# First graph layer: a sixth own-row buffer, and own rows of tile t + 1 gathered ahead of the shared rows of tile t

## Chip, cores and metric

One NeuronCore of a Trainium2 chip runs the whole program. The metric is the device time of one execution in microseconds (us). Three runs of the kernel before gave 1579.4, 1580.0 and 1585.3 us, so its median is 1580.0 us.

## What is computed

Two graph layers over 8192 nodes with 128 features each, with a random adjacency matrix of 8192 x 8192 int32 (256 MB) in which one entry in 1024 is set, so that a node has about eight neighbours.

```python
h = jnp.maximum(_layernorm(x), 0.0)
x = x + L0(h, adj, Wq, Wk)      # attention by cosine of K and Q rows, softmax over neighbours,
                                # then 0.5 * (att @ h) + 0.5 * h
h = jnp.maximum(_layernorm(x), 0.0)
x = x + L1(h, adj, W, b_W, a_vec, b_a)   # h' = h W^T + b; leaky score e_i + e_j, softmax over neighbours, att @ h'
```

Rows without a neighbour are treated apart in both layers. If a row has more neighbours than the lists hold, a flag sends the program to a dense version of both layers; with the inputs used here it isn't taken.

## The kernel before

**Tiles and rows.** The nodes are cut into T = 64 tiles of P = 128 rows. For each row the kernel finds the list of its neighbours by reading the whole adjacency matrix once (the scan). The first K = 5 neighbours of a row are its own rows: five indirect DMAs per tile, each of which gathers one table row of 130 floats into each of the 128 partitions. The neighbours beyond five are packed over the rows of a tile into shared chunks of 128; 27 chunks serve QT = 8 tiles, three or four newly gathered per tile (`GIVEN`), again one indirect DMA each.

**The scan.** The SP queue loads the adjacency matrix in pieces of 1 MB, four per tile, into a ring of six (`RING`, line 223). A piece's slot is free when TensorE has folded it (line 1091). DVE's `extract` finds the set words of a folded tile and `decode` and `compact` make its list of neighbours. Every two tiles `compact` also counts the neighbours beyond five (line 1524), and TensorE turns the counts into offsets (line 1099).

**The loop.** After a start that prepares tables and scans the first tiles, each engine runs its own hand-ordered loop over t = -1 ... 63, and semaphores tie them together:

- DVE at step t: weights of tile t - 3 (`spill_weights`, line 1585), products of the own rows of tile t - 1 (line 1568), products of its shared rows (line 1575), `select(t)`, which writes the shared index of tile t (line 1557), then offsets, `compact`, `extract`, `finish(t - 5)`, `decode`. In late steps `select(t)` stands first every second time.
- TensorE at step t: half of the folds of the scanned tile, `weighted(t - 4)` (lines 1126 and 1128), the offsets, the other folds, `owners(t + 1)` (line 1114). `weighted` counts `s_pv` up, which frees the buffers of its tile.
- ScalarE at step t: copies of owners (line 1261), scores and exponentials of tile t - 2 (line 1279), masks of tile t + 2 (lines 1247 to 1251), diagonals of tile t - 2.
- GpSimd (POOL) only issues gathers: for each t a wait for `s_pv`, five own rows (line 1029), a wait for the shared index, three or four shared rows (line 1037). Own rows land in GR = 5 buffers `G`, shared rows in a ring of CR = 20 chunks `Gc`.

At step t the scan is `lag(t)` tiles ahead. The lag falls from 8 to 4 (`LAGS`), and at each fall one step scans no tile: steps 4, 17, 30 and 43.

**After the loop** the last three tiles are finished in an order written out by hand on each engine, while the rows that the second layer reads (`second`) are normalised, projected and stored in `tab1`. The second layer (`lists_*`) starts when all are stored; POOL gathers its 536 times again (lines 540 and 545). DVE's scratch tensors of `decode` (`keyi`, `left`, `tbit`, `expo`) have space of their own, beside `keys` of `extract`.

Of the kernel before, what the change touches and what calls it, by code (L numbers as in the profile page):

```python
# [46 lines left out]
def adjacency_layers(nc, x, adj, wq, wk, w, b_w, a_vec, b_a, out):  # L47
# [4 lines left out]
    P = 128  # L52
    T = N // P
# [31 lines left out]
    DENSE_FAR = 3e38  # L85
    RING, PIECE_BITS = 6, 4
    PIECE, PIECES = PIECE_BITS * WORDS, BITS // PIECE_BITS
    GR, CR, HR, DR = 5, 20, 8, 3
    LEAD = 3
    AHEAD = 2 * LEAD  # L90

# [19 lines left out]
    with ctx:  # L111
        def sb(name, shape, dt=fp32):
            return ctx.enter_context(nc.sbuf_tensor(name, shape, dt))
# [20 lines left out]
        res = sb("res", [P, T, D])  # L134
        idx_own, idx_shared = sb("idx_own", [P, T, K], i32), sb("idx_shared", [P, NQ, C], i32)
        cnt_all, s1_all = sb("cnt_all", [P, T]), sb("s1_all", [P, T])
        none_all, some_all = sb("none_all", [P, T]), sb("some_all", [P, T])
        rstd_all, nb_all = sb("rstd_all", [P, T]), sb("nb_all", [P, T])
        hsum = sb("hsum", [P, PAIRS])
        hmean = sb("hmean", [P, 1])  # L140
# [46 lines left out]

        top = sb("top", [P, 2, 2, TOP])
        keys = sb("keys", [P, 2, HALF])
        edge_row = R[0][0:1, 0:2 * ROW].rearrange("p (a c) -> p a c", a=2)  # L190
        FLAT = 4 * TOP
        keyi, wi = sb("keyi", [P, FLAT], i32), sb("wi", [P, FLAT], i32)
        wpos = sb("wpos", [P, 2, 2 * TOP])
        left = [sb(f"left{r}", [P, FLAT])[:, :] for r in range(ROUNDS)]
        tbit = [sb(f"tbit{r}", [P, FLAT], i32) for r in range(ROUNDS - 1)]
        expo = [sb(f"expo{r}", [P, 2, 2 * TOP], i32) for r in range(ROUNDS - 1)]
        expo.append(keyi[:, :].rearrange("p (a s) -> p a s", a=2))
        cand = sb("cand", [P, 2, ROUNDS, 2 * TOP])
        got = sb("got", [P, 2, S])
# [243 lines left out]
        s_own1, s_ex_own = sem("l1_last_own_scores"), sem("l1_last_own_exp")  # L443
# [154 lines left out]
        def lists_scalar(act):  # L598
            def copy_weights(t):
                p, (first, n) = t % 2, span(t)  # L600
                act.wait_ge(s_tr1, t + 1)
                if t >= 2:
                    act.wait_ge(s_pv1, t - 1)
                for b in range(2):
                    m = min(n - 4 * b, 4)
                    if m > 0:
                        last = nc.scalar.copy(WT[p][:, 4 * b:4 * b + m, :],  # L607
                                              WT_ps[b][:, 0:m * P].rearrange("p (s c) -> p s c", s=m))
                        last.then_inc(s_WT, 1 if n > 4 else 2)
# [12 lines left out]

            def last_weights(t):
                p, (first, n) = t % 2, span(t)
                chunks = sc[p][:, K:K + n * P]
                act.wait_ge(s_sc, t + 1)
                nc.scalar.activation(chunks, chunks, ACT.Exp, bias=negm[:, p:p + 1]).then_inc(s_ex1, 1)

            def last_own_weights(t):
                p = t % 2  # L630
                act.wait_ge(s_own1, 1)
                nc.scalar.activation(own_weight[:, 0:K], sc[p][:, 0:K], ACT.Exp, bias=most[:, 1:2]).then_inc(s_ex_own, 1)
                nc.scalar.activation(own_weight[:, K:K + 1], negm[:, p:p + 1], ACT.Exp, bias=most[:, 1:2],
                                     scale=-1.0).then_inc(s_ex_own, 1)

            for t in range(AT1):
                masks1_scalar(act, t)
            for t in range(T + 1):
                if t == T:
                    last_own_weights(T - 1)  # L640
                if t >= 1:
                    copy_weights(t - 1)
                if t < T - 1:
                    own_weights(t)
                elif t == T - 1:
                    last_weights(t)
                if t + AT1 < T:
                    masks1_scalar(act, t + AT1)

        def lists_vector(dve):  # L650
# [25 lines left out]
            def last_tile(t, own, chunks, s1):  # L676
# [14 lines left out]
                nc.vector.tensor_scalar(most[:, 1:2], mine, -1.0, shift, ALU.mult, ALU.min).then_inc(s_own1, 1)  # L691
                link.add(nc.vector.tensor_tensor(rest[p], rest[p], bias[:, :], ALU.add))
                finish(t - 1)
                dve.wait_ge(s_ex_own, 2)
# [304 lines left out]
        with nc.Block() as block:  # L999
# [10 lines left out]
            def _(pool):  # L1010
# [28 lines left out]
                            in_offset=bass.IndirectOffsetOnAxis(ap=idx_shared[:, t // QT, c:c + 1], axis=0),  # L1039
                            bounds_check=None).then_inc(s_g[1][t % GR], 16)  # L1040

                for t in range(T - 1):
                    if t >= GR:
                        pool.wait_ge(s_pv, t - GR + 1)
                    gather_own(t, 0, K, s_g[0][t % GR])
                    gather_shared(t)
                pool.wait_ge(s_pv, T - GR)
                gather_shared(T - 1)
                gather_own(T - 1, 0, 3, s_g[0][(T - 1) % GR])
                gather_own(T - 1, 3, K, s_last)  # L1050
                either(pool, lambda e: None, lists_gpsimd)

            @block.tensor
            def _(pe):
# [76 lines left out]

                def weighted_last(t):
                    p, q, n = t % 2, t % GR, PAIRED[t % QT]
                    pe.wait_ge(s_W, paired(t + 1))
                    pe.wait_ge(s_fin, t - 1)
                    for j in range(n):
                        v, s, e = shared(t, SPAN[t % QT][0] + j)
                        nc.tensor.matmul(pv_ps[p][:, 0:ROW], W[p][j], Gc[:, e, :], start=j == 0, stop=False)
                    for part, (a, b) in enumerate(((0, 3), (3, K))):
                        pe.wait_ge(s_dg, t + 1 + part)  # L1140
                        for s in range(a, b):
                            last = nc.tensor.matmul(pv_ps[p][:, 0:ROW], diag[t % DR][:, s, :], G[q][:, s, :], start=False,
                                                    stop=s == K - 1)
                    last.then_inc(s_pv, 1)

                def offsets_after(i):
# [59 lines left out]
            def _(act):  # L1206
# [44 lines left out]
                    nc.scalar.activation(r, r, ACT.Relu, bias=1.0, scale=-1.0).then_inc(s_R, 1)  # L1251

                def copy_owners(t):
                    if t >= GR:
                        act.wait_ge(s_W, paired(t - GR + 1))
                    for g, chunks in enumerate(SETS[t % QT], sets(t)):
                        act.wait_ge(s_E, g + 1)
                        n, e = len(chunks), (C * (t // QT) + chunks[0]) % CR
# [131 lines left out]
                last_scores(T - 1, K, slots(T - 1), 1)  # L1390
                last_exps(T - 1, K, slots(T - 1), 3, 1)
                second.scalar_root(act, PAIRS - 3)
                second.scalar_hT(act, PAIRS - 4)
                last_scores(T - 1, 0, 3, 2)
                last_exps(T - 1, 0, 3, 6, 2)
                last_diags(T - 1, 0, 3, 2)
                second.scalar_h(act, PAIRS - 3)
                second.scalar_rows(act, PAIRS - 4)
                last_scores(T - 1, 3, K, 3)
                last_exps(T - 1, 3, K, 8, 3)  # L1400
                last_diags(T - 1, 3, K, 3)
# [13 lines left out]
            def _(dve):  # L1415
# [38 lines left out]
                def extract(t):  # L1454
# [3 lines left out]
                        dve.wait_ge(s_const, CONSTANTS)  # L1458
                    halves = keys_ps[p].rearrange("p (h c) -> p h c", h=2)
                    dve.wait_ge(s_piece, PIECES * (t + 1))  # L1460
                    a = link.add(nc.vector.max(top[:, p, 0, 0:8], halves[:, 0, :]))
                    b = link.add(nc.vector.max(top[:, p, 1, 0:8], halves[:, 1, :]))
                    link.wait(a)
# [113 lines left out]

                def spill_weights(t):
                    p = t % 2
                    dve.wait_ge(s_ex, t + 1)  # L1580
                    if t >= 2:
                        dve.wait_ge(s_pv, t - 1)
                    for j in range(PAIRED[t % QT]):
# [100 lines left out]
                spill_weights(T - 3)  # L1684
                finish(T - 5)
                dve.wait_ge(s_red, red(T - 2))
                spill_products(T - 1)
                spill_weights(T - 2)
                last_own_products(T - 1, 0, 3, s_g[0][(T - 1) % GR], go_before[(T - 1) % GR])
                finish(T - 4)  # L1690
                second.vector_stats(dve, link, PAIRS - 3)
                last_own_products(T - 1, 3, K, s_last, 32)
                finish(T - 3)
                spill_weights(T - 1)
                finish(T - 2)
# [30 lines left out]
```

## Time and profile before

| | |
|---|---|
| median of three runs | 1580.0 us |
| profiled execution, its own time | 1579.97 us |
| its span, first to last instruction | 1577.8 us |
| PE / DVE / ACT / POOL busy | 68% / 73% / 61% / 68% |
| mean granted TensorE clock | 0.839 of full speed |

The span and the time differ by 2.2 us that lie around the instructions. The program has two long stages, so the shares of the whole span say little: each stage is to be read by itself. An "issue" wait is time in which an engine waited for nothing that the profile shows.

### The profile page before, as it was taken

To read this page: it belongs to the slowest core of one execution; us is meant where nothing else is said; L and a number is where in the kernel's file an instruction comes from. 1 tells how busy PE (TensorE), PEld (TensorE's weight loads), DVE (VectorE), ACT (ScalarE), POOL (GpSimd) and SP (SyncE) were. 2 spreads that over 40 slices of the span, in tenths; PEclk is the share of its full clock that TensorE was granted. 3 is DMA by queue.
4 is the path that set the end of the run, shared out by engine and by line. 5 is a ranking of instruction groups with operands and counts; after the bars stand their busy time and mean duration, and the time that the engine had idled before them with its cause. 6 is when DMAs were issued, how large, how long until landed. Compare 5 with 4: busy or idle time off the path is not lost.

```text
span 1577.8 us, 21865 instructions
## 1 busy us (share of the span) xinstructions
PE 1078.1 (68%) x5719; PEld 811.7 (51%) x5719; DVE 1146.4 (73%) x4497; ACT 962.3 (61%) x2792; POOL 1077.7 (68%) x1121
## 2 busy tenths in 40 slices
PE   6977777798778877886865456556655665565555
PEld 4653555565556555554555345455544554454444
DVE  6995798879887888798876266666666666666667
ACT  5663867787778777787778634454445444544433
POOL 2246776677767767777666377777777777777774
PEclk9997999988989998999987667777778777877788
DMA  9999999999999999999952122222222222222222
GB/s 362 420 388 390 398 399 401 402 358 400 398 371 377 399 401 351 400 397 401 399 181 50 43 56 60 60 60 60 59 61 61 59 59 61 61 60 60 60 61 43
DMA packets 90474, 358.45 MB, mean 227 GB/s; under 512 B 23653, under 2 KB 36328, under 8 KB 57576
## 3 DMA queue, kind: packets, MB, share of 16 engines
q1 hardware_dynamic: 49128, 277.05, 44.2%
q0 software_dynamic: 34304, 71.42, 17.2%
q10 hardware_dynamic: 6912, 8.52, 1.5%
q8 instruction: 48, 0.79, 0.2%
q14 instruction: 82, 0.67, 0.1%
HBM read 344.18 MB, written 12.72 MB: 226 GB/s over the span
## 4 chain that ended last, share of the span: by engine, by line
POOL 40%; DMA 24%; issue 15%; PE 9%; DVE 7%; ACT 4%; SPq 0%; ACTq 0%; DVEq 0%; POOLq 0%
DMA arena<-in_adj_dram 20%; POOL arena L545 19%; POOL arena L540 13%; POOL arena L1029 5%; PE ps L1091 4%; POOL arena L1037 4%; DMA arena<-tab,idx_shared 3%; PE ps L1126 1%; PE ps L1114 1%; ACT prod L1279 1%; PE ps L1128 1%; DMA tab<-arena 1%; DVE norm L1443 1%; PE ps L1072 1%; DVE bst L1423 0%
## 5 line engine op out<-in xcount | busy, mean ns | idle before, releaser
L1029 POOL DMA_INDIRECT arena<-tab,idx_own x320 | 322.5, 1008 | 131.0 <-issue 92.3
L545 POOL DMA_INDIRECT arena<-tab,idx_own x320 | 303.3, 948 | 97.5 <-issue 97.5
L1091 PE MATMUL ps<-arena,fold 128*128 128x512 fp8e4 x1024 | 282.4, 411 | 105.8 <-DMA arena<-in_adj_dram 105.4
L614 ACT ACTIVATE arena<-arena,negm 128x773 f32<-128x773 f32 (+1 forms) x63 | 57.5, 913 | 357.2 <-DVE negm L743 357.2
L1037 POOL DMA_INDIRECT arena<-tab,idx_shared x216 | 209.1, 968 | 90.6 <-issue 55.9
L540 POOL DMA_INDIRECT arena<-tab,idx_shared x216 | 204.1, 945 | 87.9 <-issue 65.5
L560 PE MATMUL ps<-prod,column 128*128 128x384 f32 (+1 forms) x128 | 103.1, 905 | 227.6 <-DVE prod L657 227.6
L1091 PEld LDWEIGHTS ps<-arena,fold 128*128 128x128 bf16 x1024 | 91.1, 100 | 253.7 <-DMA arena<-in_adj_dram 149.6
L1279 ACT ACTIVATE prod<-prod,arena 128x128 f32<-128x128 f32 x528 | 203.4, 390 | 0.0
L657 DVE TENSOR_TENSOR prod<-ident,arena 128x384 f32<-128x384 f32 (+3 forms) x70 | 39.7, 574 | 216.3 <-DMA arena<-tab,idx_shared 216.3
L1114 PE MATMUL ps<-arena,R 128*128 128x154 f32 x736 | 128.1, 331 | 53.6 <-ACT R L1251 53.6
L585 PEld LDWEIGHTS ps<-arena,diag 128*128 128x128 f32 x630 | 140.2, 314 | 44.6 <-issue 40.6
L1114 PEld LDWEIGHTS ps<-arena,R 128*128 128x128 f32 x736 | 120.2, 218 | 69.9 <-ACT R L1251 56.4
L560 PEld LDWEIGHTS ps<-prod,column 128*128 128x128 f32 x128 | 28.4, 276 | 242.9 <-issue 220.9
L585 PE MATMUL ps<-arena,diag 128*128 128x130 f32 x630 | 138.2, 400 | 1.9 <-ACT diag L620 1.5
L1261 ACT COPY arena<-ps 128x308 f32<-128x308 f32 (+1 forms) x88 | 39.9, 455 | 149.9 <-PE ps L1114 147.9
L585 PE MATMUL ps<-arena 128*128 128x130 f32 x736 | 122.5, 330 | 1.4 <-ACT arena L607 1.4
L585 PEld LDWEIGHTS ps<-arena 128*128 128x128 f32 x736 | 121.0, 252 | 1.8 <-ACT arena L607 1.8
L1279 ACT ACTIVATION_READ_ACCUMULATOR prod<-prod,arena 128x1 f32 x528 | 100.5, 190 | 0.0
L620 ACT ACTIVATE diag<-ident,arena 128x128 f32<-128x128 f32 x315 | 98.9, 389 | 2.0
L1298 ACT ACTIVATE diag<-ident,weight 128x128 f32<-128x128 f32 x315 | 97.9, 386 | 0.1
L570 PE MATMUL ps<-ident,arena 128*128 128x128 f32 x368 | 56.0, 289 | 58.8 <-ACT arena L614 55.7
(220 smaller groups left out, 2505.4 us busy)
## 6 DMA issues: line engine op xcount, KB each, us to landing
arena<-in_adj_dram SPq DMA_DIRECT2D x256, 1024.0 KB, 16.4
arena<-tab,idx_own POOLq DMA_INDIRECT x640, 2.7
arena<-tab,idx_shared POOLq DMA_INDIRECT x432, 2.6
tab<-arena ACTq DMA_DIRECT2D x16, 260.0 KB, 7.3
tab<-tw ACTq DMA_DIRECT2D x32, 130.0 KB
res<-in_x_dram SPq DMA_DIRECT2D x8, 512.0 KB, 11.6
out_dram<-arena SPq DMA_DIRECT2D x64, 64.0 KB, 1.6
prod<-in_L_gnn_Wq_dram SPq DMA_DIRECT2D x1, 64.0 KB
```

The costliest lines, as they stand in the source:

```text
L540: pool.indirect_dma_start(out=GS[:, (C * h + c) % CR1, :], out_offset=None, in_=tab1, in_offset=bass.IndirectOffsetOnAxis(ap=idx_shared[:, ...
L545: pool.indirect_dma_start(out=GO[q][:, s, :], out_offset=None, in_=tab1, in_offset=bass.IndirectOffsetOnAxis(ap=idx_own[:, t, s:s + 1], ax ...
L560: last = nc.tensor.matmul(T_ps[t % 3][:, 0:n * P], column[:, 0:1].to_broadcast([P, P]), on_diag[t % 2][:, 0:n, :], start=True, stop=True)
L585: last = nc.tensor.matmul(out_ps[p][:, 0:ROW], lhs, rhs, start=s == own, stop=s == K + n - 1)
L614: nc.scalar.activation(sc[p][:, 0:K + n * P], sc[p][:, 0:K + n * P], ACT.Exp, bias=negm[:, p:p + 1]).then_inc(s_ex1, 1)
L620: last = nc.scalar.activation(diag[p][:, s, :], ident[:, :], ACT.Copy, scale=sc[p][:, s:s + 1])
L1029: pool.indirect_dma_start(out=G[t % GR][:, s, :], out_offset=None, in_=tab0, in_offset=bass.IndirectOffsetOnAxis(ap=idx_own[:, t, s:s + 1] ...
L1037: pool.indirect_dma_start(out=Gc[:, (C * (t // QT) + c) % CR, :], out_offset=None, in_=tab0, in_offset=bass.IndirectOffsetOnAxis(ap=idx_sh ...
L1091: last = nc.tensor.matmul(keys_ps[t % 2], fold[:, PIECE_BITS * f + b, :], ring8[m % RING][:, b * WORDS:(b + 1) * WORDS], start=False, stop ...
L1114: last = nc.tensor.matmul(E_ps[g % 2][:, k * REC:(k + 1) * REC], R[w % 2][:, at * P:(at + 1) * P], owner[:, w, :], start=w == of[0], stop= ...
L1279: last = nc.scalar.activation(prod[p][:, s, :], prod[p][:, s, :], ACT.Copy, scale=norm_of, accum_out=score[p][:, s:s + 1])
L1298: last = nc.scalar.activation(diag[t % DR][:, s, :], ident[:, :], ACT.Copy, scale=weight[t % 4][:, s:s + 1])
```

## The change

Own rows get six buffers in place of five. POOL gathers the own rows of tile 0, and then, for each t from 1 on, the own rows of tile t and the shared rows of tile t - 1. The wait for `s_pv` in front of the own rows keeps its form `t - GR + 1`, with GR now 6. The ring of shared chunks keeps its old guard in `copy_owners` through a new constant GC = 5. To make room, `decode`'s scratch tensors are laid over `keys`, with one more wait at the top of `extract`, and `none_all` over `code0`. Two semaphores of the second layer's last tile are dropped and two others counted further. The last tile is reordered on DVE, ScalarE and TensorE: own rows first and shared rows last.

```diff
-    GR, CR, HR, DR = 5, 20, 8, 3
+    GR, GC, CR, HR, DR = 6, 5, 20, 8, 3
...
-        none_all, some_all = sb("none_all", [P, T]), sb("some_all", [P, T])
+        none_all, some_all = code0[:, :, :, :].rearrange("p a h s -> p (a h s)"), sb("some_all", [P, T])
...
         keys = sb("keys", [P, 2, HALF])
+        scratch = keys[:, :, :].rearrange("p a (b c) -> p (a b) c", c=4 * TOP)
...
-        left = [sb(f"left{r}", [P, FLAT])[:, :] for r in range(ROUNDS)]
+        left = [scratch[:, 1 + r, :] for r in range(ROUNDS)]
...
-                act.wait_ge(s_own1, 1)
+                act.wait_ge(s_sc, T + 1)
...
-                for t in range(T - 1):
+                gather_own(0, 0, K, s_g[0][0])
+                for t in range(1, T):
                     if t >= GR:
                         pool.wait_ge(s_pv, t - GR + 1)
-                    gather_own(t, 0, K, s_g[0][t % GR])
-                    gather_shared(t)
-                pool.wait_ge(s_pv, T - GR)
+                    if t < T - 1:
+                        gather_own(t, 0, K, s_g[0][t % GR])
+                    else:
+                        gather_own(t, 0, 3, s_g[0][t % GR])
+                        gather_own(t, 3, K, s_last)
+                    gather_shared(t - 1)
                 gather_shared(T - 1)
-                gather_own(T - 1, 0, 3, s_g[0][(T - 1) % GR])
-                gather_own(T - 1, 3, K, s_last)
...
                 def weighted_last(t):
...
-                    pe.wait_ge(s_W, paired(t + 1))
                     pe.wait_ge(s_fin, t - 1)
-                    for j in range(n):
-                        v, s, e = shared(t, SPAN[t % QT][0] + j)
-                        nc.tensor.matmul(pv_ps[p][:, 0:ROW], W[p][j], Gc[:, e, :], start=j == 0, stop=False)
                     for part, (a, b) in enumerate(((0, 3), (3, K))):
                         pe.wait_ge(s_dg, t + 1 + part)
                         for s in range(a, b):
...
+                    pe.wait_ge(s_W, paired(t + 1))
+                    for j in range(n):
...
-                    if t >= GR:
-                        act.wait_ge(s_W, paired(t - GR + 1))
+                    if t >= GC:
+                        act.wait_ge(s_W, paired(t - GC + 1))
...
                     dve.wait_ge(s_piece, PIECES * (t + 1))
+                    link.wait(link.n)
...
-                    dve.wait_ge(s_ex, t + 1)
+                    dve.wait_ge(s_ex, t + (3 if t == T - 1 else 1))
...
+                last_own_products(T - 1, 0, 3, s_g[0][(T - 1) % GR], go_before[(T - 1) % GR])
+                spill_weights(T - 2)
+                last_own_products(T - 1, 3, K, s_last, 32)
+                finish(T - 4)
                 spill_products(T - 1)
-                spill_weights(T - 2)
-                last_own_products(T - 1, 0, 3, s_g[0][(T - 1) % GR], go_before[(T - 1) % GR])
-                finish(T - 4)
                 second.vector_stats(dve, link, PAIRS - 3)
-                last_own_products(T - 1, 3, K, s_last, 32)
                 finish(T - 3)
                 spill_weights(T - 1)
```

## Rows read from the trace of the kernel before

**Rows 1.** The page: the chain that ended last, its shares by line.
```profile
DMA arena<-in_adj_dram 20%; POOL arena L545 19%; POOL arena L540 13%; POOL arena L1029 5%; PE ps L1091 4%; POOL arena L1037 4%; DMA arena<-tab,idx_shared 3%; PE ps L1126 1%; PE ps L1114 1%; ACT prod L1279 1%; PE ps L1128 1%; DMA tab<-arena 1%; DVE norm L1443 1%; PE ps L1072 1%; DVE bst L1423 0%
```

**Rows 2.** Windows: stretch, length, busy us (instructions), clock, DMA share, GB/s.
```profile
core 0: us, PE busy (x) PEld busy (x) DVE busy (x) ACT busy (x) POOL busy (x), PEclk, DMA share, GB/s
...
122.00:205.00 83.00, 61.22 (x305) 37.05 (x304) 57.01 (x272) 54.35 (x173) 62.77 (x64) 0.87 1.01 392
205.00:310.00 105.00, 80.89 (x469) 56.58 (x470) 88.14 (x430) 74.03 (x255) 73.86 (x75) 0.93 1.02 401
310.00:803.00 493.00, 392.55 (x2257) 276.86 (x2256) 407.98 (x1977) 384.22 (x1329) 351.39 (x356) 0.92 0.99 388
...
891.00:1578.00 687.00, 393.47 (x1864) 323.47 (x1863) 437.17 (x1079) 312.37 (x629) 507.16 (x536) 0.75 0.26 59
```

**Rows 3.** Waits of TensorE, 205 to 803 us: total, times, longest.
```profile
PE ps L1091 <- DMA arena<-in_adj_dram: 82.5, 58, 2.9
```

**Rows 4.** Waits of POOL and of DVE, 120 to 870 us: total, times, longest.
```profile
POOL arena L1037 <- DVE idx_shared L1557: 34.7, 39, 5.9
POOL arena L1029 <- PE ps L1128: 31.2, 16, 4.6
...
DVE prod L1575 <- DMA arena<-tab,idx_shared: 71.1, 41, 4.7
```

**Rows 5.** Timeline of POOL, the first gathers of tiles 0 and 1.
```profile
122.63 1.12 POOL L1029 DMA_INDIRECT arena<-tab,idx_own  x1 [7.42 <-DMA tab<-arena]
...
129.04 0.94 POOL L1037 DMA_INDIRECT arena<-tab,idx_shared  x1 [0.30 <-issue]
...
134.04 0.94 POOL L1029 DMA_INDIRECT arena<-tab,idx_own  x1 [0.30 <-issue]
...
140.47 0.94 POOL L1037 DMA_INDIRECT arena<-tab,idx_shared  x1 [0.40 <-DVE idx_shared L1557]
```

**Rows 6.** Timeline of DVE in the same steps.
```profile
138.56 0.69 DVE L1575 TENSOR_TENSOR prod<-arena 128x512 f32<-128x512 f32 x1 [3.53 <-DMA arena<-tab,idx_shared]
...
139.94 0.25 DVE L1557 TENSOR_REDUCE idx_shared<-hit 128x4 int32<-128x96 f32 x1
...
154.69 0.16 DVE L1524 TENSOR_TENSOR spilled_to<-spilled_to,spill 128x1 f32<-128x1 f32 x1
```

**Rows 7.** Timeline of TensorE, steps 2 to 4.
```profile
155.00 0.35 PE L1099 MATMUL ps<-spill,below 128*128 128x2 f32 x2 [2.17 <-DVE spilled_to L1524]
...
157.21 1.08 PE L1091 MATMUL ps<-arena,fold 128*128 128x512 fp8e4 x4 [0.71 <-DMA arena<-in_adj_dram]
...
166.61 3.96 PE L1114 MATMUL ps<-arena,R 128*128 128x154 f32 x14 [7.01 <-ACT R L1251]
...
171.03 2.21 PE L1091 MATMUL ps<-arena,fold 128*128 128x512 fp8e4 x8
```

**Rows 8.** Timeline of the SP queue: loads of adjacency pieces, issue times.
```profile
156.53 2.12 SPq L223 DMA_DIRECT2D arena<-in_adj_dram  x2
...
172.37 5.47 SPq L223 DMA_DIRECT2D arena<-in_adj_dram  x4
```

**Rows 9.** DMA issues, 120 to 240 us, and of the whole run: median us to landing.
```profile
arena<-in_adj_dram SPq DMA_DIRECT2D x41, 1024.0 KB, 16.8
...
arena<-tab,idx_own POOLq DMA_INDIRECT x640, 2.7
```

**Rows 10.** Windows of 10 us, columns as in Rows 2.
```profile
170.00:180.00 10.00, 10.00 (x59) 6.41 (x58) 7.05 (x37) 8.63 (x30) 7.56 (x9) 0.92 1.01 394
...
320.00:330.00 10.00, 9.64 (x58) 6.54 (x57) 8.33 (x45) 8.71 (x30) 7.56 (x9) 0.91 0.81 288
...
620.00:630.00 10.00, 9.65 (x49) 7.07 (x50) 7.81 (x44) 8.60 (x34) 7.59 (x8) 0.72 0.64 203
```

**Rows 11.** Timelines of DVE and TensorE at the end of the first layer.
```profile
874.38 0.85 DVE L1585 TENSOR_SCALAR proj<-iota,arena,weight 128x128 f32<-128x128 f16 x3
...
877.02 0.16 DVE L356 TENSOR_TENSOR newton<-root 128x2 f32<-128x2 f32 x1 [1.18 <-ACT root L352]
...
878.51 1.28 PE L1142 MATMUL ps<-arena,diag 128*128 128x130 f32 x10
```

More of the change, by code:

```diff
@@ L189, in adjacency_layers @@
         keys = sb("keys", [P, 2, HALF])
+        scratch = keys[:, :, :].rearrange("p a (b c) -> p (a b) c", c=4 * TOP)
         edge_row = R[0][0:1, 0:2 * ROW].rearrange("p (a c) -> p a c", a=2)
         FLAT = 4 * TOP
-        keyi, wi = sb("keyi", [P, FLAT], i32), sb("wi", [P, FLAT], i32)
+        keyi, wi = scratch[:, 0, :].bitcast(i32), sb("wi", [P, FLAT], i32)
         wpos = sb("wpos", [P, 2, 2 * TOP])
-        left = [sb(f"left{r}", [P, FLAT])[:, :] for r in range(ROUNDS)]
-        tbit = [sb(f"tbit{r}", [P, FLAT], i32) for r in range(ROUNDS - 1)]
-        expo = [sb(f"expo{r}", [P, 2, 2 * TOP], i32) for r in range(ROUNDS - 1)]
+        left = [scratch[:, 1 + r, :] for r in range(ROUNDS)]
+        tbit = [scratch[:, 4 + r, :].bitcast(i32) for r in range(ROUNDS - 1)]
+        expo = [scratch[:, 6 + r, :].bitcast(i32).rearrange("p (a s) -> p a s", a=2) for r in range(ROUNDS - 1)]
         expo.append(keyi[:, :].rearrange("p (a s) -> p a s", a=2))
@@ L442, in adjacency_layers @@
         own_sum = Wc[:, 1:3, :].rearrange("p a c -> p (a c)")[:, 0:ROW]
-        s_own1, s_ex_own = sem("l1_last_own_scores"), sem("l1_last_own_exp")
         T_ps, WT_ps, out_ps, raw_ps = (ps[0], ps[1], ps[6]), ps[2:4], ps[4:6], ps[7]
@@ L630, in last_own_weights @@
                 p = t % 2
-                act.wait_ge(s_own1, 1)
-                nc.scalar.activation(own_weight[:, 0:K], sc[p][:, 0:K], ACT.Exp, bias=most[:, 1:2]).then_inc(s_ex_own, 1)
+                act.wait_ge(s_sc, T + 1)
+                nc.scalar.activation(own_weight[:, 0:K], sc[p][:, 0:K], ACT.Exp, bias=most[:, 1:2]).then_inc(s_ex1, 1)
                 nc.scalar.activation(own_weight[:, K:K + 1], negm[:, p:p + 1], ACT.Exp, bias=most[:, 1:2],
-                                     scale=-1.0).then_inc(s_ex_own, 1)
+                                     scale=-1.0).then_inc(s_ex1, 1)
             for t in range(AT1):
@@ L690, in last_tile @@
                 dve.wait_ge(s_sc, t + 1)
-                nc.vector.tensor_scalar(most[:, 1:2], mine, -1.0, shift, ALU.mult, ALU.min).then_inc(s_own1, 1)
+                nc.vector.tensor_scalar(most[:, 1:2], mine, -1.0, shift, ALU.mult, ALU.min).then_inc(s_sc, 1)
                 link.add(nc.vector.tensor_tensor(rest[p], rest[p], bias[:, :], ALU.add))
                 finish(t - 1)
-                dve.wait_ge(s_ex_own, 2)
+                dve.wait_ge(s_ex1, T + 2)
                 link(nc.vector.tensor_scalar(own_sum, GO[q][:, 0, :], own_weight[:, 0:1], None, ALU.mult))
@@ L1141, in weighted_last @@
                         for s in range(a, b):
-                            last = nc.tensor.matmul(pv_ps[p][:, 0:ROW], diag[t % DR][:, s, :], G[q][:, s, :], start=False,
-                                                    stop=s == K - 1)
+                            nc.tensor.matmul(pv_ps[p][:, 0:ROW], diag[t % DR][:, s, :], G[q][:, s, :], start=s == 0,
+                                             stop=False)
+                    pe.wait_ge(s_W, paired(t + 1))
+                    for j in range(n):
+                        v, s, e = shared(t, SPAN[t % QT][0] + j)
+                        last = nc.tensor.matmul(pv_ps[p][:, 0:ROW], W[p][j], Gc[:, e, :], start=False, stop=j == n - 1)
                     last.then_inc(s_pv, 1)
@@ L1389, in _ @@
                 second.scalar_rows(act, PAIRS - 5)
-                last_scores(T - 1, K, slots(T - 1), 1)
-                last_exps(T - 1, K, slots(T - 1), 3, 1)
+                last_scores(T - 1, 0, 3, 1)
+                last_exps(T - 1, 0, 3, 3, 1)
+                last_diags(T - 1, 0, 3, 1)
                 second.scalar_root(act, PAIRS - 3)
                 second.scalar_hT(act, PAIRS - 4)
-                last_scores(T - 1, 0, 3, 2)
-                last_exps(T - 1, 0, 3, 6, 2)
-                last_diags(T - 1, 0, 3, 2)
+                last_scores(T - 1, 3, K, 2)
+                last_exps(T - 1, 3, K, K, 2)
+                last_diags(T - 1, 3, K, 2)
                 second.scalar_h(act, PAIRS - 3)
                 second.scalar_rows(act, PAIRS - 4)
-                last_scores(T - 1, 3, K, 3)
-                last_exps(T - 1, 3, K, 8, 3)
-                last_diags(T - 1, 3, K, 3)
+                last_scores(T - 1, K, slots(T - 1), 2 + len(runs(T - 1)))
+                last_exps(T - 1, K, slots(T - 1), slots(T - 1), 3)
                 second.scalar_hT(act, PAIRS - 3)
```

## The prediction

> **What bounds the kernel now.** I read the chain of waits first. It is shared by the loads of the adjacency matrix and by POOL's gathers, those of the first layer (lines 1029 and 1037) and those of the second (540 and 545) [rows 1]. That mixes two stages, so I cut the span into windows [rows 2]. From 205 to 803 us the DMA engines are full: share 1.02 and 401 GB/s up to 310 us, 0.99 and 388 GB/s after it. From 891 us on they are a quarter busy and POOL gathers without a pause; the change leaves that stage alone, apart from which semaphore counts a sixth buffer, so its 687 us stay.
>
> In the first stage two things could set the pace: the stream of 1 MB loads, or POOL with 8 or 9 gathers per tile. TensorE's waits decide: its folds stood 58 times for an adjacency piece that had not landed [rows 3]. POOL waited too, 34.7 us for shared indices and 31.2 us for TensorE to free own buffers [rows 4], but an engine that waits is not late. Over most of this stage the stream is the bound: whatever brings loads forward shortens the kernel, whatever lets the stream fall dry lengthens it.
>
> The third view is the start of the loop. There POOL is the late one: it issues back to back from 122.63 us, one gather every 1.25 us ((134.04 - 129.04) / 4), and the reader should see that the shared rows of tile 1 at 140.47 came 0.40 us after POOL was free: its own rows fill exactly the time in which the shared rows of tile 0 land and DVE selects [rows 5, 6].
>
> **The change, part by part.**
>
> *Own rows one tile ahead.* No gather is added or dropped. Look at what stands in the POOL queue between the shared rows of tile k - 1 and those of tile k: five own rows, before and after. Before they belong to tile k and wait until `s_pv` is k - 4. After, they belong to tile k + 1 and wait until `s_pv` is (k + 1) - 6 + 1, which is k - 4 again. So the sixth buffer pays for the tile of lead, and in the steady loop POOL does the same work behind the same waits. `select(k)` still stands on DVE behind the products of the shared rows of tile k - 1 (line 1575), which is what DVE waited for, 71.1 us in all [rows 4]; the own rows landed before them in any case. Steady loop: 0. Bounds: nothing gained, and at most what the stream has lost after 310 us, (401 - 388) / 401 x 493 = 16.0 us [rows 2]. I take 0, because the gates are the same. A rule speaks against that: POOL's wait for a free own buffer repeats, 16 times [rows 4], and the Trainium skill (Perfetto Trace Analysis, section Optimization Strategy) says that a gap which repeats on the engine that should be saturated can mean too little room for the next tile, its buffer count among the causes. By that rule the sixth buffer would close the gap and the term would be up to -16.0 in place of 0, the faster rival below; the trace agrees on the gap, but shows the DMA engines as the ones that are saturated there.
>
> *The start.* Here the order costs. POOL gathers the own rows of tile 0, now those of tile 1 too, and only then the shared rows of tile 0, whose index was there already (the gather at 129.04 waited for nothing but its issue [rows 5]). That is 5 x 1.25 = 6.25 us later. What is queued behind it, followed through the engines: the shared products of tile 0 at 138.56 and the index of tile 1 at 139.94 move by 6.25 us [rows 6]; POOL meanwhile gathers own rows of tile 2, as it gathered those of tile 1 before, so the shift is neither made up nor made larger. One step on, `compact` writes the counts at 154.69 [rows 6], and TensorE stood 2.17 us for exactly that count, at 155.00 [rows 7]. It will now stand until 161.25. Behind it wait the folds of line 1091; the second of them had waited 0.71 us for its piece at 157.21, which swallows as much: 6.25 - 0.71 = 5.54 us are left. They pass through the owners, ScalarE's masks and the next owners at 166.61 to the folds at 171.03 [rows 7], since step 4 scans no tile and nothing else stands there.
>
> A fold frees a slot of the ring, so the load that was issued at 172.37 [rows 8] goes out at 177.9. Is the stream dry by then? The two loads before it were issued at 156.53 and within the 2.12 us behind it, the later at about 158.3. Loads landed 16.8 us after issue (median), so it lands near 175.1; 41 loads in 120 us are one per 2.93 us, so the next one is due at 178.0 [rows 8, 9]. A load issued on engines that have run dry takes, as an estimate, those 2.93 us and the 2.7 us in which a lone small gather lands [rows 9], 5.6 us together: issued at 172.37 it landed just in time, and the window of that time shows no loss, share 1.01 and 394 GB/s [rows 10]. There is no slack left, so the delay is paid nearly whole. Bounds: 0 if pieces in flight cover it, 5.54 if they cover nothing; the nearest rows are the two windows in which the stream did fall dry, with 288 and 203 GB/s [rows 10], so I go near the upper end: 5.0, as gathers under way in the dry stretch land sooner and give some of it back. After that the stream is the bound as before, all later, and nothing gives the 5.0 us back.
>
> *The last tile.* ScalarE does the same instructions in another order. DVE's six W of the last tile were done at 875.2 (874.38 + 0.85), before the last own diagonals; now they come after the last exponential, six at 0.85 / 3 each, 1.7 us, and TensorE's ten own matmuls, 1.28 us at 878.51, move in front and run beside them [rows 11]. 1.7 - 1.28 = 0.4. `finish(62)` and the statistics at 877.02, which had waited for ScalarE, now stand behind these W as well. Bounds 0 and 1.7; I take 0.5. That POOL issues its last gather some 6 us sooner gains nothing, for it waits there for the stored rows of the second layer, which ScalarE's order sets.
>
> *Edits at nothing.* Scratch over `keys` and `none_all` over `code0` move addresses only. The wait at the top of `extract` is DVE's for its own last instruction; hidden, because DVE has 71.1 us of waits for gathers in the loop [rows 4]. Without that cover it is at most one short instruction, 0.16 us (as at 154.69), for each of some 57 tiles: 9 us. GC = 5 leaves the old guard. The two counted-on semaphores release at the same instructions as those dropped.
>
> **Sum.** 0 + 5.0 + 0.5 + 0 = 5.5 us on the profiled execution's 1579.97: **1585.5 us**. The median of the runs, 1580.0, is the same, so the forecast is 0.35% more, inside the 0.5% (7.9 us) below which a measurement of this kernel can't tell a change from none.
>
> **Rivals.**
>
> *The start is swallowed (0.22).* If pieces in flight cover the late load, or the masks at 166.61 have slack that I don't see, only the 0.5 us remain: 1580.5. For it: share 1.01 in 170 to 180 us. Against: TensorE's 2.17 us wait, which is zero slack.
>
> *Faster, 1569.5 (0.13).* POOL's waits do cost the stream, at the steps that scan no tile, where the loop must do two steps within one tile of loads and POOL is what it waits for. If own rows fetched a tile earlier let the loop run through them, the 16.0 us of lost stream come back: 1579.97 - 16.0 + 5.5 = 1569.5. It decides from 13.4 us regained (7.9 + 5.5). For it: the holes at 320 and 620 us [rows 10] and 31.2 us in which POOL stood for a free own buffer [rows 4]. Against: the same gate k - 4.
>
> *Clearly slower, 1590.4 (0.15).* A stream that falls dry loses more than the delay, since its refill is thin: in the hole at 620 us it lost (401 - 203) / 401 x 10 = 4.9 us [rows 2, 10]. Once more on top of the 5.0 us, between 175 and 190 us: 1585.5 + 4.9 = 1590.4. It decides from 7.4 us lost at the start. Against: in the hole after 320 us loads filled the ring again without a second hole.
>
> **How the numbers follow.** The forecast has the remaining 0.50, with 1583 to 1588 (the start between 2.5 and 7.4). The range leaves out the faster rival and half of the slower: 1577 to 1591. Faster by over 0.5%: 0.12, nearly all of that rival. Slower by over 0.5% (over 1587.9): the slower rival and a little of the forecast's upper end, 0.19. Within 0.5%: 0.69.
>
> **What would show it.** In the profile after: the first shared gather near 135.3; the wait for line 1524 near 161; the load of 172.37 near 178 and a window with a DMA share clearly under 1 at 175 to 185; the same two POOL waits in the steady loop, still near 35 and 31 us; the same second layer, later by 5 us. The prediction is wrong if the first load after the gap is late but its window is full, or if POOL's waits for own buffers vanish and the stream ends before 803 us.

## The result and the profile after

| kernel | median, us | runs (lowest to highest) | ratio to before, 95% interval |
|---|---|---|---|
| before | 1579.72 | 11 (1578.88 to 1585.30) | |
| after | 1585.55 | 11 (1582.96 to 1589.24) | 1.0034 [1.0026, 1.0042] |

The forecast was 1585.5 us, no change within 0.5%; the ratio makes it 0.0034 x 1579.72 = 5.4 us more. That the median came within 0.05 us of the forecast is luck: the interval alone is 2.5 us wide. The profiled execution of after took 1587.66 us (span 1585.5), 2.1 us over its median. One execution of a kernel reported below (five buffers, new last tile) took 4947.56 us, with TensorE busy 99% of its span; its ratio leaves it out, and no profile of that kernel is used.

First the windows of after, with the columns of [rows 2]: three of 10 us at the start of the loop, then the stages.

```profile
core 0: us, PE busy (x) PEld busy (x) DVE busy (x) ACT busy (x) POOL busy (x), PEclk, DMA share, GB/s
160.00:170.00 10.00, 5.88 (x22) 3.62 (x22) 7.99 (x35) 3.86 (x19) 7.82 (x8) 0.67 1.02 402
170.00:180.00 10.00, 6.88 (x25) 4.88 (x26) 7.92 (x43) 7.73 (x26) 7.59 (x8) 0.58 0.53 182
180.00:190.00 10.00, 10.00 (x72) 7.72 (x70) 5.86 (x29) 9.07 (x33) 7.73 (x8) 1.00 1.00 379
122.00:205.00 83.00, 58.41 (x277) 34.35 (x275) 51.25 (x243) 47.80 (x152) 62.92 (x65) 0.80 0.94 364
205.00:310.00 105.00, 79.47 (x462) 54.53 (x462) 91.06 (x450) 77.83 (x268) 74.32 (x75) 0.93 1.02 400
310.00:808.00 498.00, 393.89 (x2266) 277.41 (x2264) 407.00 (x1965) 382.79 (x1314) 356.37 (x354) 0.91 0.99 385
897.00:1585.00 688.00, 397.64 (x1864) 326.58 (x1864) 437.25 (x1079) 312.91 (x629) 506.50 (x536) 0.74 0.27 59
```

Compare the second line with [rows 10]: in the same 10 us the DMA share was 1.01 and is 0.53, 394 GB/s became 182. That is the hole, and it is new. Over 122 to 205 us the core moved 364 GB/s where it had moved 392 [rows 2]: (392 - 364) / 392 x 83 = 5.9 us of stream. The 105 us after it are as before, and the second layer too. From 310 us on this execution ran at 385 GB/s instead of 388, about 4 us more. Two runs below, one with the same start (the start alone) and one with the lead from tile 15 on, have 390 there, so neither part was seen to cost it; it may belong to the one execution that was profiled, which is slower than its median.

Now how the hole comes about, engine by engine. POOL, the first gathers of own rows of tiles 0 and 1 and of shared rows of tiles 0 and 1 (the answer to [rows 5]):

```profile
122.15 1.12 POOL L1029 DMA_INDIRECT arena<-tab,idx_own  x1 [7.75 <-DMA tab<-arena]
...
128.57 0.94 POOL L1029 DMA_INDIRECT arena<-tab,idx_own  x1 [0.30 <-issue]
...
134.81 0.94 POOL L1037 DMA_INDIRECT arena<-tab,idx_shared  x1 [0.30 <-issue]
...
146.24 0.94 POOL L1037 DMA_INDIRECT arena<-tab,idx_shared  x1 [0.40 <-DVE idx_shared L1560]
```

DVE: the shared products of tile 0, the index of tile 1, the counts (the answer to [rows 6]):

```profile
144.33 0.69 DVE L1578 TENSOR_TENSOR prod<-arena 128x512 f32<-128x512 f32 x1 [9.63 <-DMA arena<-tab,idx_shared]
...
145.72 0.25 DVE L1560 TENSOR_REDUCE idx_shared<-hit 128x4 int32<-128x96 f32 x1
...
159.92 0.16 DVE L1527 TENSOR_TENSOR spilled_to<-spilled_to,spill 128x1 f32<-128x1 f32 x1
```

TensorE (the answer to [rows 7]), and the SP queue with the loads that were issued at 156.53 and 172.37 before [rows 8]:

```profile
160.22 0.56 PE L1101 MATMUL ps<-spill,below 128*128 128x2 f32 x2 [8.32 <-DVE spilled_to L1527]
...
161.07 3.57 PE L1093 MATMUL ps<-arena,fold 128*128 128x512 fp8e4 x8
...
173.12 3.96 PE L1116 MATMUL ps<-arena,R 128*128 128x154 f32 x14 [7.01 <-ACT R L1253]
...
177.54 2.40 PE L1093 MATMUL ps<-arena,fold 128*128 128x512 fp8e4 x8
```

```profile
162.97 2.03 SPq L224 DMA_DIRECT2D arena<-in_adj_dram  x2
...
179.07 5.41 SPq L224 DMA_DIRECT2D arena<-in_adj_dram  x4
```

Follow the delay down these rows. POOL started 0.48 us earlier in this execution, so the shared products are 144.33 - 138.56 = 5.77 us late, which is 6.25 - 0.48. The counts are 5.23 us late, TensorE's wait ends 5.22 us late (it was 2.17 us long and is 8.32), the owners at 173.12 and the folds at 177.54 are 6.51 us late, the load 6.70 us. The hole itself ends when that load arrives:

```profile
160.00:173.00 13.00, 5.88 (x22) 3.62 (x22) 10.85 (x52) 6.76 (x24) 10.21 (x10) 0.63 1.01 400
173.00:180.00 7.00, 6.88 (x25) 4.88 (x26) 5.06 (x25) 4.82 (x21) 5.20 (x6) 0.61 0.34 92
```

The waits of the loop, POOL's (120 to 875 us), TensorE's (205 to 808 us) and DVE's (120 to 875 us): total, times, longest.

```profile
POOL arena L1029 <- PE ps L1130: 36.7, 16, 4.9
POOL arena L1037 <- DVE idx_shared L1560: 26.2, 35, 5.4
```

```profile
PE ps L1093 <- DMA arena<-in_adj_dram: 80.8, 58, 2.8
```

```profile
DVE prod L1578 <- DMA arena<-tab,idx_shared: 71.5, 36, 9.6
```

POOL still waits for own buffers 16 times, and TensorE 58 times for a piece [rows 3, 4]. The sixth buffer has not taken POOL's wait away.

### The profile page after: what moved, and what is told of

The parts are those of the page before. It is cut to its first block, busy times and chain, and to the rows that moved or that the text cites. A ratio compares the mean times of both kernels' runs of the same rounds, so it can differ in the third digit from the quotient of the medians.

```text
span 1585.5 us, 21927 instructions
## 1 busy us (share of the span) xinstructions
PE 1081.0 (68%) x5719; PEld 810.9 (51%) x5719; DVE 1146.0 (72%) x4497; ACT 963.1 (61%) x2792; POOL 1083.5 (68%) x1121
## 4 chain that ended last, share of the span: by engine, by line
POOL 41%; DMA 26%; issue 15%; PE 10%; ACT 4%; DVE 4%; SPq 0%; ACTq 0%; DVEq 0%; POOLq 0%
DMA arena<-in_adj_dram 23%; POOL arena L545 18%; POOL arena L540 13%; POOL arena L1029 6%; POOL arena L1037 4%; PE ps L1093 4%; DMA arena<-tab,idx_shared 2%; ACT prod L1281 1%; PE ps L1074 1%; PE ps L1116 1%; PE ps L1128 1%; DMA tab<-arena 1%; PE ps L1080 1%; PE ps L1130 1%; PE ps L1062 0%
## 5 line engine op out<-in xcount | busy, mean ns | idle before, releaser
L1093 PE MATMUL ps<-arena,fold 128*128 128x512 fp8e4 x1024 | 286.3, 415 | 101.8 <-DMA arena<-in_adj_dram 101.4
L1116 PE MATMUL ps<-arena,R 128*128 128x154 f32 x736 | 124.8, 325 | 53.6 <-ACT R L1253 53.6
```

The source lines that it names most:

```text
L1093: last = nc.tensor.matmul(keys_ps[t % 2], fold[:, PIECE_BITS * f + b, :], ring8[m % RING][:, b * WORDS:(b + 1) * WORDS], start=False, stop ...
L1116: last = nc.tensor.matmul(E_ps[g % 2][:, k * REC:(k + 1) * REC], R[w % 2][:, at * P:(at + 1) * P], owner[:, w, :], start=w == of[0], stop= ...
```

## The experiments

Each kernel was timed in five rounds beside the kernel before on the same chip. Its median there was 1580.17 us for the first four runs, 1579.65 for the next four, 1580.99 for the last two. The ratios and intervals are those on record. They are not the quotients of the medians beside them and differ from these by up to 0.0013: the start alone has 1.0045, where 1585.21 / 1580.17 is 1.0032.

Theory: the whole loss is made in the first 180 us, by the order of the first gathers, and the rest of the change is worth nothing. Rivals: the lead, the sixth buffer's gates, the last tile or the extract's wait takes part in it.

**After, with the order of before up to tile 14.** Only then the lead begins.

```
gather_own(0, 0, K, s_g[0][0])
for t in range(1, LATE + 1):        # LATE = 14
    gather_shared(t - 1)
    if t >= GC:
        pool.wait_ge(s_pv, t - GC + 1)
    gather_own(t, 0, K, s_g[0][t % GR])
for t in range(LATE + 1, T):        # as in after
```

> The kernel after, but the lead of the own rows begins only at tile 14: up to there the queue stands as before (own rows of t, shared rows of t), then the own rows of 14 and 15 follow each other, where POOL waits for the stream anyway. Theory (the order at the start costs the time, the lead itself costs and gains nothing): 1580.0 to 1581 us, like before plus 0.5 for the last tile; no window under a DMA share of 0.9 between 170 and 190 us. Rival (the lead in the steady loop, the wait in extract or the last tile costs it): still 1584 to 1587 us. Rival (the lead is worth something and the start hid it): below 1577 us.

Measured: 1580.28 us, ratio 1.0004 [0.9994, 1.0013]. Its window at the start and, below, POOL's two waits (120 to 870 us):

```profile
122.00:205.00 83.00, 62.19 (x291) 37.18 (x291) 55.16 (x259) 51.95 (x169) 60.86 (x62) 0.82 1.00 390
```

```profile
POOL arena L1037 <- DVE idx_shared L1566: 30.5, 39, 5.4
POOL arena L1029 <- PE ps L1136: 27.4, 18, 3.7
```

390 GB/s: all but a trace of the hole is gone (from 170 to 180 us the share is 0.92, where after had 0.53), and with it the loss, while the lead runs for the other 49 tiles with the new last tile and the extract's wait. Together they neither cost nor give anything that can be measured.

**Before, with the new start alone.**

```diff
-for t in range(T - 1):
+gather_own(0, 0, K, s_g[0][0])
+gather_own(1, 0, K, s_g[0][1])
+gather_shared(0)
+gather_shared(1)
+for t in range(2, T - 1):
```

> The kernel before, with one thing changed: own rows of tiles 0 and 1, then shared rows of tiles 0 and 1, then everything as before; five buffers, no lead afterwards, the old last tile. Theory: the same 6.25 us delay of the first shared rows, so 1585 us (4.5 to 6 more than before) with the hole in the stream near 175 to 180 us. Rival (the cost sits in the lead, the sixth buffer, extract or the last tile): 1580 us.

Measured: 1585.21 us, ratio 1.0045 [1.0031, 1.0059]. Its windows:

```profile
122.00:205.00 83.00, 58.93 (x274) 35.47 (x273) 48.42 (x230) 46.87 (x148) 56.67 (x58) 0.79 0.91 352
...
170.00:180.00 10.00, 5.19 (x17) 3.95 (x18) 8.11 (x37) 7.73 (x26) 7.83 (x8) 0.53 0.38 120
```

Five gathers in another place, in a kernel that is otherwise that of before, make a hole at the same place and the whole loss.

**How much delay costs how much.** Three more starts on the kernel before: two of the five own gathers of tile 1 moved ahead of the shared rows of tile 0; own rows of tiles 0, 1 and 2 ahead of them; and the shared rows of tile 0 ahead of everything.

```diff
+gather_own(0, 0, K, s_g[0][0])
+gather_own(1, 0, K // 2, s_g[0][1])
+gather_shared(0)
+gather_own(1, K // 2, K, s_g[0][1])
+gather_shared(1)
```

> The kernel before with only two of the five own gathers of tile 1 moved ahead of the shared rows of tile 0: a delay of about 2.5 us for them instead of 6.25. If the delay less the 0.71 us of slack that the prediction allowed passes on, the loss is about 1.8 us: 1582.0, ratio 1.0011. If the outstanding loads have more slack than that, as the whole loss of 4.75 us for a delay of 6.25 at the piece at 172 us could also be read (1.5 us of slack), the loss is 1.0 us: 1581.2, ratio 1.0006. If the loss is one fixed gap it is 4 to 5 us: 1585, ratio 1.003.

```diff
+for t in range(3):
+    gather_own(t, 0, K, s_g[0][t])
+for t in range(3):
+    gather_shared(t)
```

> The kernel before with nothing changed but the start of its gathers: own rows of tiles 0, 1 and 2, then shared rows of tiles 0, 1 and 2, so that the first shared gather starts 12.5 us later instead of 6.25. If the stream's delay passes on in full, as the prediction has it, the second 6.25 us cost as much again or all of their size: 1590 to 1592 us, ratio 1.006 to 1.008, with a dry stretch of about 11 us in the windows of 170 to 190 us. The rival, that the loss is one fixed gap at the turn to the first folds whatever the delay, says 1585, ratio 1.003 to 1.004.

```diff
+gather_shared(0)
+gather_own(0, 0, K, s_g[0][0])
+for t in range(1, T - 1):
```

> The kernel before with the four shared gathers of tile 0 ahead of the own gathers of tile 0, so that the shared rows come about 6 us earlier. The windows before show the load stream full from 24 to 310 us, so my theory, that the start only loses where the stream falls dry, says no change: 1580.2 us, ratio 0.9995 to 1.0005. A rival, that the time follows the date of the shared gathers both ways, says 5 us less: 1575, ratio 0.997.

Measured: 1581.99 us, ratio 1.0025 [1.0015, 1.0035], for two own gathers ahead; 1592.03 us, 1.0086 [1.0072, 1.0100], for two tiles ahead; 1581.70 us, 1.0012 [1.0002, 1.0021], for shared rows first. The windows of the first two, the last three lines fitted to the holes of the second:

```profile
122.00:205.00 83.00, 61.31 (x281) 36.16 (x280) 52.93 (x254) 50.08 (x162) 59.68 (x61) 0.81 0.96 373
...
170.00:180.00 10.00, 9.24 (x44) 6.94 (x44) 7.73 (x41) 7.76 (x27) 7.87 (x8) 0.65 0.59 195
```

```profile
122.00:205.00 83.00, 55.85 (x253) 32.69 (x253) 45.85 (x216) 42.76 (x137) 51.99 (x54) 0.76 0.86 329
...
165.00:171.00 6.00, 3.58 (x11) 1.85 (x12) 5.79 (x34) 0.00 (x0) 4.47 (x6) 0.50 0.32 100
172.00:177.00 5.00, 1.20 (x10) 0.97 (x8) 3.42 (x15) 3.76 (x18) 3.55 (x4) 0.82 0.98 393
178.00:187.00 9.00, 6.79 (x25) 4.79 (x26) 7.16 (x38) 6.76 (x23) 6.44 (x7) 0.58 0.23 53
```

With the double delay there are two holes, with a full stretch between them. In the table, the second column is the time from POOL's first gather to DVE's products of the shared rows of tile 0, less the 15.93 us of before (138.56 - 122.63); the third is the stream lost in 122 to 205 us, (392 - GB/s) / 392 x 83; the last is the ratio less 1, times the median of before beside it, with the ends of its interval. The second and third columns come from one profiled execution each, the last from all runs; in the starts that lose no time the third column still has 0.4 and 1.3 us, which is its noise.

| start | products later by, us | stream lost in that window, us (GB/s) | time lost, us |
|---|---|---|---|
| six buffers, order of before (below) | 0.0 | 1.3 (386) | -0.8 [-2.2, 0.6] |
| after, up to tile 14 as before | 0.5 | 0.4 (390) | 0.6 [-0.9, 2.1] |
| shared rows first | 1.0 | 2.8 (379) | 1.9 [0.3, 3.3] |
| two own gathers ahead | 2.8 | 4.0 (373) | 3.9 [2.4, 5.5] |
| after | 6.3 | 5.9 (364) | 5.4 [4.1, 6.6] |
| the start alone | 7.1 | 8.5 (352) | 7.1 [4.9, 9.3] |
| own rows of two tiles ahead | 12.7 | 13.3 (329) | 13.6 [11.4, 15.8] |

The loss follows the delay about one for one, and the lost stream of one window gives it back within 2.1 us in each row. By differences of medians the last column would read -1.4, 0.1, 2.1, 2.3, 5.8, 5.0 and 12.4 us, so one for one is the size and not a law, and after and the start alone are not told apart. The theory of a fixed gap is out (1.0086 for the double delay). On slack the half delay does not decide: 3.9 [2.4, 5.5] us lies above the 1.8 us expected with 0.71 us of slack, but 2.3 us by the medians does not lie far from it. Part of the spread is made on the way: the load that went out at 172.37 in before went out at 177.10 with two own gathers ahead and at 181.11 with the start alone, 4.7 and 8.7 us late.

With shared rows first, no change was expected, and it came out a little slower. DVE had no use for the early rows: its products of tile 0 begin with the own rows, which now came second.

```profile
124.65 1.12 POOL L1037 DMA_INDIRECT arena<-tab,idx_shared  x1 [9.35 <-DVE idx_shared L1559]
...
140.75 0.89 DVE L1570 TENSOR_TENSOR prod<-arena 128x384 f32<-128x384 f32 x2 [11.58 <-DMA arena<-tab,idx_own]
141.56 0.69 DVE L1577 TENSOR_TENSOR prod<-arena 128x512 f32<-128x512 f32 x1
```

So it is the last row that tile 0 needs that counts. The order also made POOL itself start late: its first gather stood for the index of tile 0 until 124.65, where before began own rows at 122.63. The table counts from that first gather and leaves these 2.0 us out; on the clock the shared products are 141.56 - 138.56 = 3.0 us late. An earlier start could not have been shown to gain anyway, as the stream before was full.

**After, with five own buffers.** The lead stays, its buffer goes.

```diff
-GR, GC, CR, HR, DR = 6, 5, 20, 8, 3
+GR, GC, CR, HR, DR = 5, 5, 20, 8, 3
```

> The kernel after with GR = 5: the lead stays, the sixth buffer goes. The own rows in front of the shared rows of tile k then wait until s_pv is k - 3 in place of k - 4. Theory (the sixth buffer only pays for the lead): POOL's waits for TensorE grow from 37 us to over 150 us, the loop falls behind the stream, and the time is over 1620 us. Rival (own buffers were not short): 1585 to 1588 us.

Measured: 1807.75 us, ratio 1.1450 [1.1434, 1.1466]. The waits of POOL (120 to 990 us), TensorE and DVE (205 to 990 us), and the window of the loop:

```profile
POOL arena L1029 <- PE ps L1130: 252.4, 32, 13.4
```

```profile
PE ps L1101 <- DVE spilled_to L1527: 243.0, 24, 13.1
```

```profile
DVE prod L1578 <- DMA arena<-tab,idx_shared: 267.2, 31, 13.4
```

```profile
310.00:990.00 680.00, 428.75 (x2316) 298.07 (x2315) 417.91 (x2033) 393.72 (x1362) 354.88 (x364) 0.79 0.79 291
```

Three waits of about 250 us that close a ring: POOL waits for TensorE, TensorE for DVE's counts, DVE for POOL's rows. The chain that ended last goes round it between 400 and 439 us: from POOL's gathers to DVE, from DVE's counts to TensorE, and back to POOL. The gate in front of the shared rows of tile k is now `s_pv` at k - 3 instead of k - 4; with one tile less in flight the loop runs at its own latency, and the stream at 291 GB/s. So the sixth buffer pays for the lead, and as the gates of before and after are the same, nothing of it is left over in after. The time is far over the 1620 us that was expected at the least.

**After, with six buffers and the order of before.** Here the sixth buffer is free for POOL: own rows may go a tile earlier, shared rows keep their gate.

```diff
-gather_own(0, 0, K, s_g[0][0])
-for t in range(1, T):
+for t in range(T):
     if t >= GR:
         pool.wait_ge(s_pv, t - GR + 1)
     ...
-    gather_shared(t - 1)
-gather_shared(T - 1)
+    if t >= GC:
+        pool.wait_ge(s_pv, t - GC + 1)
+    gather_shared(t)
```

> The kernel after with the order of before in POOL's loop (own rows of t, then shared rows of t) and six buffers, so that the own rows of k wait only until s_pv is k - 5; the shared rows keep their guard k - 4 by a wait of their own. The start is that of before. Theory (the stream is the bound): 1578 to 1581 us, POOL's wait for TensorE merely moves to the shared rows or to the index. Rival (POOL's waits for a free buffer cost the stream at the steps without a scan): 1566 to 1574 us.

Measured: 1578.76 us, ratio 0.9995 [0.9986, 1.0004]. No change that can be told.

**The rest of the change, taken apart.** The same with five buffers (what stays is the last tile, the temporaries and the extract's wait); six buffers and the extract's wait without the new last tile; and the temporaries and the extract's wait alone. The edit that tells the last two apart is this one:

```diff
-GR, GC, CR, HR, DR = 6, 5, 20, 8, 3
+GR, GC, CR, HR, DR = 5, 5, 20, 8, 3
...
-                    if t >= GC:
-                        pool.wait_ge(s_pv, t - GC + 1)
```

> The changed kernel with five own-row buffers again and with the order of the kernel before for the gathers (own rows of tile t, then shared rows of tile t); what stays of the change is the last tile's new order, the decoder's temporaries over the keys and the extract's added wait. The prediction's terms (0.5 us for the last tile, nothing for the wait and the temporaries) say 1580.7 us beside a kernel before of 1580.2, ratio 1.0003. The rival, from the profile of the changed kernel, where the last store of the first layer to the first gather of the second takes some 1.6 us less, says 1578.6 us, ratio 0.999. An extract wait that is not hidden would show as up to 9 us more (1589).

> The kernel before with six own-row buffers, the decoder's temporaries over the keys and the extract's added wait, with the shared rows still gated by the end of the tile five back and the order of the gathers and of the last tile as in the kernel before. Theory one, that the load stream sets the first layer and POOL's waits for own buffers (31 us in all before) are cover: no change, 0.9995 to 1.0005 of the kernel before. Theory two, from setting the run with six buffers, the old order and the new last tile (0.9995) beside the run with five buffers and the same (1.0009): the sixth buffer gives about 2 us, ratio 0.9985, and this version is under both kernels, near 1577.8 us.

> The same with five own-row buffers: of the change only the decoder's temporaries over the keys and the wait that it puts in front of each tile's extract. The prediction's term is nothing: 1.0000, 0.9995 to 1.0005. The rival: the 0.0009 that the last tile, the temporaries and the wait cost together is the wait, since TensorE's waits for line 1527 are longer with it; then 1.0009, some 1.4 us, and the last tile costs nothing.

| | five buffers | six buffers, gates of their own |
|---|---|---|
| new last tile | 1580.38 us, 1.0009 [1.0000, 1.0018] | 1578.76 us, 0.9995 [0.9986, 1.0004] |
| last tile of before | 1581.90 us, 1.0004 [0.9993, 1.0014] | 1580.91 us, 0.9994 [0.9984, 1.0003] |

Every one of the four is within 0.1% of the kernel before. Down the columns, the last tile is worth 0.0005 and 0.0001, 0.8 and 0.2 us; along the rows, the sixth buffer -0.0014 and -0.0010, about -2 us. The last tile's two are below half an interval, so nothing is shown there. The sixth buffer's two are a little above it and have one sign, but a difference of two runs is less certain than each, so a gain of some 2 us is neither shown nor excluded: 0.9994 [0.9984, 1.0003] holds both the 0.9985 and the 1 of the two theories. In the same way the 1.0004 of the temporaries and the wait holds the 1.0000 of the theory and the 1.0009 of its rival. What it did to POOL is plain, in POOL's waits (120 to 870 us) of the run with six buffers and the last tile of before:

```profile
POOL arena L1037 <- DVE idx_shared L1560: 69.2, 44, 5.4
...
POOL arena L1037 <- PE ps L1130: 3.8, 5, 1.3
POOL arena L1029 <- PE ps L1130: 0.9, 3, 0.3
```

and in two windows of 10 us of the same run, whose lines before are in [rows 10]:

```profile
320.00:330.00 10.00, 8.36 (x44) 4.97 (x45) 7.72 (x44) 8.71 (x30) 6.97 (x7) 0.84 0.79 280
620.00:630.00 10.00, 8.76 (x51) 6.37 (x50) 8.95 (x51) 8.57 (x32) 7.40 (x9) 0.88 0.86 310
```

POOL's 31.2 us of waits for TensorE [rows 4] are down to 3.8 + 0.9 = 4.7 us, and its waits for shared indices are up from 34.7 to 69.2 us. The wait has moved to the next instruction of the queue, and the stream from 310 to 803 us runs at 388 GB/s, as in [rows 2]. The two holes are still there, 280 and 310 GB/s where before had 288 and 203; the second is as shallow, 307, in the run with the lead from tile 15 on, which has the gates of before, so POOL's wait for own buffers did not make them.

No version was shown to beat the kernel before; the one with six buffers, the old order and the new last tile is the best median, but its interval holds 1.

## Why the prediction was right

*Steady loop, 0.* Right. With the lead from tile 15 on and the old start the time is that of before (1.0004), and with five buffers the lead costs 1807.75 - 1580.17 = 228 us: the gate k - 4 was the point. The two POOL waits are 36.7 and 26.2 us, 62.9 in all, where they were 65.9 [rows 4]; the prediction had each near its old value, and they moved by 5.5 and 8.5 us against each other, which the time does not show.

*The start, 5.0.* Right in its place and its path; measured 5.4 [4.1, 6.6] for the whole change, 7.1 [4.9, 9.3] for the start alone (by the medians 5.8 and 5.0); the intervals overlap, and what lies between was not resolved. Its size was in part luck. Between the counts and the folds the prediction took 0.71 us off, since a fold had waited that long for its piece. That wait did vanish (eight folds run in one piece at 161.07), but the delay grew from 5.22 to 6.51 us on this way, by 1.29. The same 22 matmuls from the counts to the owners took 3.89 us of TensorE before and 5.88 in after, 1.99 more, and their granted clock was 1.00 before and 0.61 in after:

```profile
155.00:159.60 4.60, 3.89 (x22) 2.46 (x22) 4.46 (x18) 3.58 (x8) 3.60 (x4) 1.00 1.02 401
```

```profile
160.20:166.10 5.90, 5.88 (x22) 3.61 (x22) 4.49 (x18) 0.00 (x0) 4.68 (x5) 0.61 1.01 393
```

1.99 less the 0.71 of the vanished wait is the growth of 1.3. Between the two levels, 1.2 and 2.4 GHz, a mean of 0.61 is 2 x (1 - 0.61) = 78% of the stretch at the lower one. So the load went out 6.70 us late, at 179.07, not 5.54 us, at 177.9. Against this stand 5.9 us of lost stream and 5.4 us of time: the refund that the prediction allowed, 0.5 us, could be in the difference of 0.8, since the DMA engines moved 92 GB/s in the hole, but this is no more than the noise of that column. A delay that was sized too small and a time that lies somewhat under the delay met near 5.0.

One step was missed without harm. The prediction left the two loads before, of 156.53 and about 158.3, in their place, but their slots too are freed by folds behind the counts: in after they went out from 162.97 on, and the stream stayed full until 173 even so. With the double delay they went out from 170.16 on, and that is the first of its two holes, from 165 to 171 us.

*The last tile, 0.5.* Not contradicted: 0.8 and 0.2 us in the two pairs, below what was resolved. The six W do stand in the chain now, after the last exponential, as the chain of waits of after shows; the first two lines are theirs:

```profile
886.37 0.86 DVE Wc L1588 x3
887.23 0.77 DVE proj L1588 x3
...
896.54 2.50 DMA tab<-tw
```

They take 0.86 + 0.77 = 1.63 us, the 1.7 us of the prediction's upper bound. The last line is what it did not think of: the store that the second layer's first gather waits for landed in 2.50 us in this execution, and in 4.23 us in the profiled one of before. Why was not tried.

*Edits at nothing.* 1.0004 [0.9993, 1.0014] for the temporaries and the extract's wait: nothing that can be told, and far from the 9 us that the wait could have cost uncovered (0.6%).

*The rivals.* The start was not swallowed. The clearly slower one is not the case of after: its bound was 7.4 us at the start, and the 10 us behind the hole are full (share 1.00). The start alone, 7.1 [4.9, 9.3], does not exclude that size, and a delay twice as long does come to 1592, with two holes. The faster one is out as far as it was tried: the run with six buffers and the last tile of before took POOL's wait for own buffers away, and got 0.9994 instead of the 16 us, with the holes at 320 and 620 us still there. The Trainium skill (Perfetto Trace Analysis, section Optimization Strategy) says that a gap which repeats on the engine that should be saturated can mean too few buffers. What is saturated here is the DMA engines, and the gap stood on POOL, so the trace does not contradict the rule but its use on POOL.

## What to carry to other kernels

Before a reordering is judged by its steady loop, write down the first three trips of the loop by hand: a gather that is early for the next tile is late for the first one, and where a stream runs full with hardly a spare load in flight, a late start is paid about once, and here it was not earned back. A ring that grows by one buffer and a lead that grows by one tile cancelled; look at which count each wait compares with. A wait that an extra buffer removed from an engine off the path turned up as the next wait of the same queue.

## What the runs showed of the hardware

The stream of 1 MB loads had little slack, although a load took 16.8 us to land [rows 9] and its ring holds six: 2.8 us of delay at DVE cut the DMA share of 170 to 180 us from 1.01 to 0.59. And TensorE's granted clock can lengthen a delay that waits for TensorE: the 22 matmuls from the counts to the owners took 3.89 us at a clock of 1.00 (before), 5.54 at 0.72 (temporaries and wait alone), 5.88 at 0.61 (after), 6.59 at 0.54 (the start alone) and 6.69 at 0.53 (two own gathers ahead). TensorE had stood 2.17, 2.38, 8.32, 8.98 and 4.89 us in front of them. The clock was lowest behind long waits, but 2.38 us was followed by 0.72 where 2.17 was followed by 1.00, so that the standing is what lowers it is not shown.
